# A redrawn first phase, and eight row blocks of the second graph layer done with seven block products instead of eight

## The chip, the cores and the metric

The kernel runs on one core of a Trainium2 chip. Its time is device time in microseconds (us) of one execution. Before the change the median of three runs is 610.74 us (609.37 to 611.44). Engines are named as the profile names them: PE is TensorE's matmul, PEld its weight load, DVE VectorE, ACT ScalarE, POOL GpSimd, SP the queue that issues most transfers.

## The reference, cut to what matters

There are 3327 nodes with 256 features and a dense symmetric 0/1 adjacency `adj` with about 1% ones. Two residual graph layers follow each other, each on `h = relu(layernorm(x))`:

```python
# layer 0 (adj_a = adj_b = adj)
attn_a = sigmoid([adj @ h, h] @ Wa.T + ba); attn_b = sigmoid([adj @ h, h] @ Wb.T + bb)
g = h @ W_sa;  e = where(adj != 0, exp(-leaky_relu(s_left[:, None] + s_right[None, :], 0.01)), 0)
x = x + sigmoid(attn_a * (e / (e.sum(1) + 1e-5)) @ g + attn_b * (adj @ (h @ W_gcnb) + b_gcnb))
# layer 1, h taken anew from x
a_norm = dinv * (adj + I) * dinv
x = x + relu((a_norm @ h + h) @ W + b)
```

## The kernel before, in words

Nodes are padded to 26 tiles of 128, handled as 13 pairs (`PAIRS`); a pair has tiles e = 0, 1. `m` is a pair of output rows and `u` the pair of nodes that is summed over. Every fp32 operand of a product is split into a 16-bit first half and a 16-bit rest (`HI` and `LO`, `HI1` and `LO1`, `Z` read as bf16 and `E2`), so one product costs two or three matmuls. Order within an engine is written by hand and engines meet at semaphores only.

*First phase.* For s = 0..12 PE runs `dense(s)` (h times both weight matrices, 12 matmuls of 512 columns into `accA[1]`), `turn(s + 2)` (four fp32 transposes), for s from 6 on `neighbours(0, s - 6)`, from 7 on `unit(0, s - 7)`, and `project(s + 1)` (8 matmuls of 18 or 12 columns, each with its own weights). DVE takes the mean and variance of x (`row_stats`), makes the second halves (`turned_second`, `second_halves`) and the scores; POOL makes the inverse deviations in eight batches (`BATCHES`), a batch when all its pairs' statistics are there; ACT normalises. `load_adj(m, c)` on POOL brings the adjacency rows of pair m in two chunks (6 and 7 pairs wide) into `stage`, and `turn_adj(m, c)` on DVE turns a chunk with two stream transposes into `adjT[m % 2]`; a load waits until the chunk before it in the same place has been turned.

*Layer 0.* For every m and u, ACT makes `leaky` and `expo` of 128x512 scores, DVE `mask` (times the adjacency) and `split`, PE `unit(m, u)` (12 matmuls of 257 or 256 columns into `accE`) and, for the next m, `neighbours(m + 1, u - 6)` (8 matmuls of 260 or 258 columns). A ring of 8 buffers of `Z` lets ACT and DVE run ahead. Between m = 0 and m = 1 PE runs all of `neighbours(1, u)` and then waits in `unit(1, 0)` for `row_sums(0)` on DVE, which empties `accE` and adds what `with_bias(0)` on POOL has made. `with_bias(0)` stands behind `load_adj(3, 0)` and the small operation `nbias` in POOL's order.

*Layer 1.* `dense1(m)` makes h times W for pair m (`HI1`, `LO1`). `pooled(k, u)` adds four tiles' products for output pair `ORDER[k]`: 8 matmuls of 256 columns, 104 for one k. The transposed adjacency comes back from `adjT_store` into three buffers `adj1[k % 3]`. POOL makes the node's own term (`self_term(k)`: add, two scalings, add), DVE adds it (`pooled_out`), takes relu and residual and ACT issues the store. Blocks k = 0, 1, 2 are interleaved while the last `dense1` are made, k = 3..11 follow each other, and k = 12 is done tile by tile (`pooled_tile`).

Of the kernel before, what the change touches and what calls it, by code (L numbers as in the profile page):

```python
# [12 lines left out]
P = 128  # L13
QUAD = 32
# [5 lines left out]
def gnn_kernel(nc, x, adj, W_sa, a_sa, W_g, b_g, Wa, ba, Wb, bb, W1, b1, out):  # L20
# [14 lines left out]
    BATCHES = [(0, 1), (1, 2), (2, 3), (3, 4), (4, 5), (5, 7), (7, 9), (9, PAIRS)]  # L35
# [6 lines left out]

    def chunk_of(u):
        return [c for c, (a, b) in enumerate(CHUNKS) if a <= u < b][0]

    def batch_of(i):
        return [n for n, (a, b) in enumerate(BATCHES) if a <= i < b][0]

# [3 lines left out]
    with ExitStack() as ctx:  # L52
# [100 lines left out]

        def bank(t, e):
            return t[:, 512 * e:512 * e + 512]
# [94 lines left out]
        tile_done = sem("tile_done")  # L250
        y_ok = sem("y_ok")
        o_ok = sem("o_ok")
        o_out = [sem("o_out0"), sem("o_out1")]

# [30 lines left out]
        def _(sp):  # L285
# [20 lines left out]
            def keep_adj(m):  # L306
                sp.wait_ge(tr_ok, NC * (m + 1))
                sp.dma_start(adjT_store[m], adjT[m % 2][:].rearrange("p u e i v -> p (u e i v)").bitcast(U32)
                             ).then_inc(stored[m % 2], 16)
# [3 lines left out]

            sp.wait_ge(adj_in[1], adj_count(1, 1))
            spread_left(0)
# [19 lines left out]
            sp.wait_ge(tr_ok, NC * PAIRS)  # L335
# [11 lines left out]
        def _(pool):  # L347
# [9 lines left out]
            def load_adj(m, c):  # L357
                u0, u1 = CHUNKS[c]
                if m >= 1:
                    pool.wait_ge(tr_ok, NC * (m - 1) + c + 1)  # L360
# [15 lines left out]
            def inv_stds(n):  # L376
                a, b = BATCHES[n]
                pool.wait_ge(stats, b)
                pool.tensor_tensor(ve[:, a:b], mv[:, a:b, :, 1], epss[:, 0:b - a], ALU.add).then_inc(vplus, 1)
                pool.wait_ge(vplus, n + 1)  # L380
                pool.tensor_tensor(rstd[:, a:b], ve[:, a:b], halfs[:, 0:b - a], ALU.pow).then_inc(rstd_ok, 1)
# [33 lines left out]
            inv_stds(0)  # L415
            inv_stds(1)
            pool.wait_ge(pads, 1)
            load_adj(0, 0)
            inv_stds(2)
            score_weight_parts()  # L420
            load_adj(0, 1)
            loads = {6: (1, 0), 7: (1, 1), 11: (2, 0), 12: (2, 1)}
            for s in range(PAIRS):
                score_parts(s)
                if s == 0:
                    inv_stds(3)
                if s in (0, 1, 2, 4):
                    inv_stds({0: 4, 1: 5, 2: 6, 4: 7}[s])
                gate_columns(s)
                if s in loads:  # L430
                    load_adj(*loads[s])

# [27 lines left out]
            pool.wait_ge(bias_in, 32)  # L460
            pool.tensor_scalar(nbias[:], bias2[:], -1.0, None, ALU.mult).then_inc(nbias_ok, 1)
# [13 lines left out]
            def self_term(k):  # L475
# [6 lines left out]
                pool.wait_ge(hp_ok, k + 1)  # L482
                pool.wait_ge(selfw_ok, 1)
                for e in range(2):
                    t = 2 * ORDER[k] + e
                    ins = pool.tensor_scalar(hpw[:, e], hp[:, e], selfw[:, t:t + 1], None, ALU.mult)
                ins.then_inc(hpw_c, 1)
# [3 lines left out]

            for k in range(PAIRS):
                self_term(k)

        @block.scalar
        def _(act):
# [8 lines left out]
            def norm(i):  # L505
                act.wait_ge(x_in[group_of(i)], x_count(group_of(i)))
                act.wait_ge(nmr_ok, batch_of(i) + 1)
# [6 lines left out]
            def turned(i):  # L514
                act.wait_ge(hT_ps, i + 1)
                if i >= 2:
                    act.wait_ge(dn_ps, 2 * i - 2)
# [8 lines left out]
            def first_halves(i):  # L526
                src = dn[:].rearrange("p (e k d) -> p e k d", e=2, k=2)
                for e in range(2):
                    act.wait_ge(dn_ps, 2 * i + e + 1)
                    dst = bass.AP(HI[:].tensor, (2 * i + e) * HIW, [[TILES * HIW, P], [G0, 2], [1, D]])  # L530
                    act.activation(dst, src[:, e], ACT.Copy).then_inc(hi_ok, 1)
# [79 lines left out]
            for s in range(PAIRS + 7):  # L611
                if s == 0:
                    first_halves(0)
                if s + 1 < PAIRS:
                    turned(s + 1)
                if s + 2 < PAIRS:
                    norm(s + 2)
                if 0 <= s - 6 < PAIRS:
                    expo(0, s - 6)
                if 0 < s < PAIRS:  # L620
                    first_halves(s)
                if s == 1:
                    left_first()
                if 0 <= s - 5 < PAIRS:
                    leaky(0, s - 5)
                if s == 11:
                    first_weights(2)
            act.wait_ge(srw_ok, PAIRS)
            act.activation(el[:], srw[:, :, 3], ACT.Exp, scale=SLOPE).then_inc(el_ok, 1)
            gate_exp(0)  # L630
            gated_b(0)

            for m in range(1, PAIRS):
                for u in range(PAIRS + 1):
                    if u == 1 and m >= 2:
                        norm1(m - 2)
                    if u == 2 and m >= 2:
# [3 lines left out]
                    if u == 7:  # L641
                        half_tanh(m - 1)
                    if u == 9:
                        gate_exp(m)
                    if u == 12:
# [3 lines left out]
                    if u >= 1:  # L649
                        expo(m, u - 1)  # L650
            norm1(LAST - 1)
# [5 lines left out]
            rounded1(LAST)  # L657
            first_halves1(LAST)

# [19 lines left out]

            for k in range(PAIRS):  # L680
                store_out(k)
            act.wait_ge(o_out[0], out_count(LAST, 0))
# [3 lines left out]
        def _(pe):  # L686
# [42 lines left out]
            def dense(i):  # L729
# [3 lines left out]
                for e in range(2):  # L733
                    if i >= 1:
# [14 lines left out]
            def neighbours(m, u):  # L749
                if u in [a for a, _ in CHUNKS]:  # L750
                    pe.wait_ge(tr_ok, NC * m + chunk_of(u) + 1)
# [82 lines left out]

            def pooled_tile(k, e):
# [21 lines left out]
            for s in range(PAIRS):  # L857
                dense(s)
                if s == 0:
                    turn(1)  # L860
                    project(0)
                    spread_weights(2, 4, 2)
                    keep_busy(4)
                if s == 1:
                    widen_first()
                if s + 2 < PAIRS:
# [3 lines left out]
                if s >= 6:  # L870
                    neighbours(0, s - 6)
                if s >= 7:
                    unit(0, s - 7)
                if s + 1 < PAIRS:
                    project(s + 1)
            for u in range(PAIRS - 6, PAIRS):
                neighbours(0, u)
                unit(0, u - 1)
            unit(0, LAST)
            for u in range(PAIRS):  # L880
# [26 lines left out]
            for u in range(2, 5):  # L907
                pooled(2, u)
            dense1(LAST)
            for u in range(5, 8):  # L910
# [6 lines left out]
            for k in range(3, LAST):  # L917
                for u in range(PAIRS):
                    pooled(k, u)
            for e in range(2):  # L920
# [3 lines left out]
        def _(dve):  # L924
# [15 lines left out]
            def minus_mean(n):  # L940
                a, b = BATCHES[n]
                dve.wait_ge(rstd_ok, n + 1)
                dve.scalar_tensor_tensor(out=nmr[:, a:b], in0=mv[:, a:b, :, 0], scalar=-1.0, in1=rstd[:, a:b],
# [61 lines left out]
            def second_halves(i):  # L1005
                for e in range(2):
                    dve.wait_ge(hi_ok, 2 * i + e + 1)
                    first = bass.AP(HI[:].tensor, (2 * i + e) * HIW, [[TILES * HIW, P], [G0, 2], [1, D]])
                    dve.tensor_tensor(LO[:, 2 * i + e, 0:2 * D].rearrange("p (k d) -> p k d", k=2),
                                      bank(dn, e).rearrange("p (k d) -> p k d", k=2), first,  # L1010
                                      ALU.subtract).then_inc(lo_ok, 1)

            def turn_adj(m, c):
# [9 lines left out]
                for e in range(2):  # L1023
                    src = stage[:, e].bitcast(U32).rearrange("p b (u r) -> p b u r", r=QUAD)[:, :, u0:u1]
# [246 lines left out]
```

## Time and profile before

| | |
|---|---|
| median of three runs | 610.74 us |
| the profiled execution, its own time | 611.8 us |
| its span in the profile | 610.0 us |
| granted TensorE clock, mean over the span | 0.993 |
| PE / PEld busy | 593.4 / 508.4 us |
| DVE / ACT / POOL busy | 425.2 / 362.4 / 255.5 us |

The 1.8 us between the execution's own time and its span lie around the profile. PE busy counts pipelined matmuls with their whole latency, so how much PE does is better read from the spacing of starts; where the timeline shows starts at an even spacing, that spacing is the cost of one.

### The profile page before, as it was taken

To read this page: it belongs to the slowest core of one execution; us is meant where nothing else is said; L and a number is where in the kernel's file an instruction comes from. 1 tells how busy PE (TensorE), PEld (TensorE's weight loads), DVE (VectorE), ACT (ScalarE), POOL (GpSimd) and SP (SyncE) were. 2 spreads that over 40 slices of the span, in tenths; PEclk is the share of its full clock that TensorE was granted. 3 is DMA by queue.
4 is the path that set the end of the run, shared out by engine and by line. 5 is a ranking of instruction groups with operands and counts; after the bars stand their busy time and mean duration, and the time that the engine had idled before them with its cause. 6 is when DMAs were issued, how large, how long until landed. Compare 5 with 4: busy or idle time off the path is not lost.

```text
span 610.0 us, 13250 instructions
## 1 busy us (share of the span) xinstructions
PE 593.4 (97%) x5265; PEld 508.4 (83%) x5265; DVE 425.2 (70%) x811; ACT 362.4 (59%) x878; POOL 255.5 (42%) x361
## 2 busy tenths in 40 slices
PE   7889998999999999999999999999999999999996
PEld 5446687888888888888888888888888888888886
DVE  6897885999998999899989989988753121111111
ACT  3687667797887979797979788979642000000000
POOL 3664313554453435343525276313132374435433
PEclk8999999899999999999999999999999999999999
DMA  8908399957566565647474745010400486546401
GB/s 198 225 3 113 111 134 249 203 83 182 94 150 121 123 134 110 146 98 162 81 177 67 190 52 79 2 19 1 130 2 18 113 318 215 174 157 193 144 20 35
DMA packets 55801, 73.60 MB, mean 121 GB/s; under 512 B 20027, under 2 KB 47933, under 8 KB 54331
## 3 DMA queue, kind: packets, MB, share of 16 engines
q0 software_dynamic: 28544, 22.15, 26.5%
q1 hardware_dynamic: 24754, 46.42, 23.5%
q10 hardware_dynamic: 2441, 4.20, 2.2%
q8 instruction: 41, 0.67, 0.4%
q14 instruction: 21, 0.17, 0.1%
HBM read 69.31 MB, written 22.16 MB: 150 GB/s over the span
## 4 chain that ended last, share of the span: by engine, by line
PE 82%; DVE 5%; DMA 4%; issue 4%; POOL 4%; ACT 2%; ACTq 0%; POOLq 0%; DVEq 0%
PE accE L786 11%; PE accE L788 11%; PE accE L787 11%; PE accA L764 10%; PE accA L765 10%; PE accA L831 7%; PE accA L830 7%; PE accE L830 4%; PE accE L831 4%; DMA stage<-in_adj_dram 3%; POOL stage L369 1%; DVE bst L933 1%; PE pw L803 1%; PE accA L847 1%; PE pw L805 1%
## 5 line engine op out<-in xcount | busy, mean ns | idle before, releaser
L786 PE MATMUL accE<-HI,Z 128*128 128x257 f16 x676 | 185.2, 274 | 2.4 <-DVE wm L1078 2.1
L788 PE MATMUL accE<-HI,E 128*128 128x257 f16 x676 | 184.8, 273 | 0.0
L787 PE MATMUL accE<-LO,Z 128*128 128x256 f16 x676 | 184.7, 273 | 0.0
L549 ACT ACTIVATE Z<-LO,sr 128x256 f32<-128x256 f32 x338 | 151.4, 497 | 35.6 <-PE accE L788 35.6
L764 PE MATMUL accA<-HI,adjT 128*128 128x260 f16 x676 | 154.0, 273 | 0.0
L765 PE MATMUL accA<-LO,adjT 128*128 128x258 f16 x676 | 154.0, 273 | 0.0
L558 ACT ACTIVATE Z<-Z,sr 128x256 f32<-128x256 f32 x338 | 150.1, 496 | 0.2
L1034 DVE TENSOR_TENSOR Z<-adjT,Z 128x512 f32<-128x512 bf16 x169 | 127.0, 751 | 17.1 <-ACT Z L558 16.1
L1040 DVE TENSOR_TENSOR E<-Z 128x512 bf16<-128x512 f32 x169 | 129.0, 763 | 5.8
L369 POOL DMA_DIRECT2D stage<-in_adj_dram x96 | 59.3, 649 | 93.0 <-DVE adjT L1026 88.6
L831 PE MATMUL accA<-LO,adjT 128*128 128x256 f16 x416 | 91.6, 273 | 0.0
L830 PE MATMUL accA<-HI,adjT 128*128 128x256 f16 x416 | 91.6, 273 | 0.0
L786 PEld LDWEIGHTS accE<-HI,Z 128*128 128x128 bf16 x676 | 66.0, 98 | 11.6 <-issue 2.3
L764 PEld LDWEIGHTS accA<-HI,adjT 128*128 128x128 bf16 x676 | 65.8, 97 | 9.2
L787 PEld LDWEIGHTS accE<-LO,Z 128*128 128x128 bf16 x676 | 66.2, 98 | 8.7
L788 PEld LDWEIGHTS accE<-HI,E 128*128 128x128 bf16 x676 | 66.0, 98 | 8.8
L765 PEld LDWEIGHTS accA<-LO,adjT 128*128 128x128 bf16 x676 | 65.8, 97 | 8.8
L1026 DVE STREAM_TRANSPOSE adjT<-stage 128x768 uint32<-128x768 uint32 (+1 forms) x52 | 51.0, 1017 | 1.1 <-DMA stage<-in_adj_dram 1.1
L448 POOL TENSOR_SCALAR wx<-wx 128x512 f32<-128x512 f32 x13 | 12.6, 968 | 81.8 <-ACT wx L584 81.8
L830 PE MATMUL accE<-HI,stage 128*128 128x256 f16 x208 | 45.7, 273 | 0.0
L831 PE MATMUL accE<-LO,stage 128*128 128x256 f16 x208 | 45.7, 272 | 0.0
L830 PEld LDWEIGHTS accA<-HI,adjT 128*128 128x128 bf16 x416 | 40.7, 98 | 4.7
(127 smaller groups left out, 721.0 us busy)
## 6 DMA issues: line engine op xcount, KB each, us to landing
adjT_store<-adjT SPq DMA_DIRECT2D x11, 1664.0 KB, 6.3
stage<-in_adj_dram POOLq DMA_DIRECT2D x48, 192.0 KB, 5.0
stage<-in_adj_dram POOLq DMA_DIRECT2D x36, 224.0 KB, 5.2
adjT<-adjT_store SPq DMA_DIRECT2D x7, 896.0 KB, 6.0
adjT<-adjT_store SPq DMA_DIRECT2D x7, 768.0 KB, 6.0
stage<-adjT_store SPq DMA_DIRECT2D x4, 896.0 KB, 6.4
stage<-adjT_store SPq DMA_DIRECT2D x4, 768.0 KB, 5.8
out_dram<-late ACTq DMA_DIRECT2D x11, 256.0 KB
```

The source lines that it names most:

```text
L369: pool.dma_start(stage[32 * b:32 * b + 32, :, :, w0:w1_], src).then_inc(adj_in[c], 16)
L549: ins = act.activation(Z[:, n % RING, v], slw[:, m], ACT.Relu, bias=sr99[:, t:t + 1], scale=1.0 - SLOPE)
L558: ins = act.activation(Z[:, n % RING, v], Z[:, n % RING, v], ACT.Exp, bias=sr01[:, t:t + 1], scale=-1.0)
L764: pe.matmul(dst[:, 0:D + 4], w, HI[:, t, ONE:HIW], start=(t == 0), stop=False)
L765: ins = pe.matmul(dst[:, 2:D + 4], w, LO[:, t, D:LOW], start=False, stop=(t == TILES - 1))
L786: pe.matmul(dst[:, 0:D + 1], zhi, HI[:, t, 0:D + 1], start=(t == 0), stop=False)
L787: pe.matmul(dst[:, 0:D], zhi, LO[:, t, 0:D], start=False, stop=False)
L788: ins = pe.matmul(dst[:, 0:D + 1], zlo, HI[:, t, 0:D + 1], start=False, stop=(t == TILES - 1))
L830: pe.matmul(dst, w, HI1[:, t, :], start=(t == 0), stop=False)
L831: ins = pe.matmul(dst, w, LO1[:, t, :], start=False, stop=(t == TILES - 1))
L1034: dve.tensor_tensor(Z[:, n % RING], rows, Z[:, n % RING], ALU.mult).then_inc(mask_ok, 1)
L1040: dve.tensor_tensor(E2[:, n % RING], Z[:, n % RING], hi, ALU.subtract).then_inc(e2_ok, 1)
```

## The change

The first phase is put in another order. Statistics are made pair by pair (`inv_std(i)`, `minus_mean(i)`, one `row_stats` a step, four ahead). The second half of `dense(0)` and `dense(1)` comes behind `turn(1)` and `turn(2)`, `project(0)`. `turn_adj` does one transpose at a time and stands at steps 4 to 7 and 11 to 14. `unit(0, u)` moves from step u + 7 to u + 10, `neighbours` stay at u + 6; the steps go on to 22 and take `neighbours(1, 0..3)` with them. `nbias` moves to the front of POOL's order; `gate_args(0)`, `gates(0)`, both chunks of `turn_adj(2, ·)` and `row_sums(0)` go into the loop over u of m = 1 (at u = 1, 3, 2 and 4, 7 and 9, and 6).

In layer 1 the blocks k = 4..11 (`SEVEN`) take two pairs of nodes (a "duo", 6 of them) as a 2x2 block product: two output tiles, two summed pairs, two halves of 128 columns. Seven products of 128 columns stand in the place of eight, by sums made beforehand: `TH`, `TL` of the node values (once), `SA` of the adjacency (per block: three sums on DVE, one on POOL, in two parts). The thirteenth pair keeps its 8 matmuls of 256 columns. `output_seven` puts the products together. The scaling in the own term moves from POOL to ACT.

```diff
-            def inv_stds(n):
-                a, b = BATCHES[n]
-                pool.wait_ge(stats, b)
+            def inv_std(i):
+                pool.wait_ge(stats, i + 1)
...
             pool.wait_ge(consts, 5)
-            inv_stds(0)
-            inv_stds(1)
+            inv_std(0)
+            inv_std(1)
             pool.wait_ge(pads, 1)
             load_adj(0, 0)
-            inv_stds(2)
+            inv_std(2)
             score_weight_parts()
             load_adj(0, 1)
-            loads = {6: (1, 0), 7: (1, 1), 11: (2, 0), 12: (2, 1)}
+            pool.wait_ge(bias_in, 32)
+            pool.tensor_scalar(nbias[:], bias2[:], -1.0, None, ALU.mult).then_inc(nbias_ok, 1)
+            inv_std(3)
+            inv_std(4)
+            loads = {6: (1, 0), 8: (1, 1)}
...
+            def adj_difference(k, part):
+                adj_sums_wait(pool, k, part)
+                w0, w1 = PARTS[part]
+                pool.tensor_tensor(combos(k, 2, w0, w1), duo_adj(k, 0, 0, w0, w1), duo_adj(k, 0, 1, w0, w1),
+                                   ALU.subtract).then_inc(s3_ok, 1)
+
             for k in range(PAIRS):
+                if k + 1 in SEVEN:
+                    for part in range(2):
+                        adj_difference(k + 1, part)
                 self_term(k)
...
+            def pooled_seven(k):
+                pe.wait_ge(y_ok, 2 * (k - 2))
...
+                        for n, (weights, hi, lo) in enumerate((
+                                (adjs[0], HI1[:, ta, H[0]], LO1[:, ta, H[0]]),
+                                (adjs[1], HI1[:, tb, H[0]], LO1[:, tb, H[0]]),
+                                (sums[3], HI1[:, tb, H[1]], LO1[:, tb, H[1]]),
+                                (sums[1], TH[:, b, v, H[1]], TL[:, b, v, H[1]]),
+                                (adjs[3], TH[:, b, v, H[0]], TL[:, b, v, H[0]]),
+                                (None, None, None),
+                                (sums[0], TH[:, a, v, H[0]], TL[:, a, v, H[0]]),
+                                (sums[2], TH[:, a, v, H[1]], TL[:, a, v, H[1]]))):
...
-            turns = {5: (0, 0), 6: (0, 1), 10: (1, 0), 11: (1, 1)}
+            turns = {4: (0, 0, 0), 5: (0, 0, 1), 6: (0, 1, 0), 7: (0, 1, 1),
+                     11: (1, 0, 0), 12: (1, 0, 1), 13: (1, 1, 0), 14: (1, 1, 1)}
...
+            def adj_sums(k, part):
+                n = 2 * (k - SEVEN[0]) + part + 1
+                adj_sums_wait(dve, k, part)
+                w0, w1 = PARTS[part]
+                dve.tensor_tensor(combos(k, 0, w0, w1), duo_adj(k, 0, 1, w0, w1), duo_adj(k, 1, 1, w0, w1),
+                                  ALU.add).then_inc(s1_ok, 1)
...
+            for k in SEVEN:
+                output_seven(k)
+                if k + 2 in SEVEN:
+                    for part in range(2):
+                        adj_sums(k + 2, part)
```

## Rows read from the trace of the kernel before

**Rows 1.** The page: busy time of each engine; a group of ACT (busy us, mean ns).
```profile
PE 593.4 (97%) x5265; PEld 508.4 (83%) x5265; DVE 425.2 (70%) x811; ACT 362.4 (59%) x878; POOL 255.5 (42%) x361
...
L549 ACT ACTIVATE Z<-LO,sr 128x256 f32<-128x256 f32 x338 | 151.4, 497 | 35.6 <-PE accE L788 35.6
```
**Rows 2.** Waits of PE: who was waited for, us in total, times, longest.
```profile
PE tp L690 <- DVE hTx L990: 3.0, 5, 0.9
PE accE L786 <- DVE wm L1078: 2.1, 1, 2.1
```
**Rows 3.** PE's timeline in layer 1 (start, length): blocks 3 to 11, then 12.
```profile
491.55 0.27 PE L830 MATMUL accA<-HI,adjT 128*128 128x256 f16 x1
...
593.73 0.27 PE L846 MATMUL accA<-HI,adjT 128*128 128x256 f16 x1
```
**Rows 4.** PE's timeline in step 5 and 6 of the first phase.
```profile
39.67 0.63 PE L690 MATMUL tp<-ident,hf 128*128 128x128 f32 x4 [0.67 <-DVE hTx L990]
40.14 0.17 PE L718 MATMUL pw<-w6s,hTx 128*128 128x18 bf16 x1
...
40.34 0.38 PE L738 MATMUL accA<-wh,hTx 128*128 128x512 f16 x1
...
42.71 0.38 PE L740 MATMUL accA<-wh,hTx 128*128 128x512 f16 x1
```
**Rows 5.** Weight loads in the same 0.2 us, PEld's timeline.
```profile
40.17 0.10 PEld L718 LDWEIGHTS pw<-w6s,hTx 128*128 128x128 f16 x1
40.19 0.10 PEld L720 LDWEIGHTS pw<-w6s,hTx 128*128 128x128 f16 x1
```
**Rows 6.** Groups of DVE by line, 12 to 50 us: busy us, mean ns of one.
```profile
L1009 DVE TENSOR_TENSOR LO<-accA,HI 128x512 f16<-128x512 f32 x16 | 10.3, 682 | 1.3 <-ACT HI L531 1.3
L933 DVE BATCH_NORM_STATS2 bst<-xs 128x6 f32<-128x256 f32 x22 | 8.2, 411 | 0.0
L1026 DVE STREAM_TRANSPOSE adjT<-stage 128x768 uint32<-128x768 uint32 (+1 forms) x4 | 3.9, 1018 | 0.0
```
**Rows 7.** PE's timeline: first matmul of `dense(7)` and of `dense(12)`.
```profile
45.21 0.38 PE L738 MATMUL accA<-wh,hTx 128*128 128x512 f16 x1
...
73.01 0.38 PE L738 MATMUL accA<-wh,hTx 128*128 128x512 f16 x1
```
**Rows 8.** Between m = 0 and 1: DVE's, POOL's and ACT's timelines.
```profile
89.37 1.84 DVE L1026 STREAM_TRANSPOSE adjT<-stage 128x768 uint32<-128x768 uint32 x2 [1.09 <-DMA stage<-in_adj_dram]
91.50 2.39 POOL L369 DMA_DIRECT2D stage<-in_adj_dram  x4 [12.16 <-DVE adjT L1026]
94.28 0.48 ACT L567 ACTIVATE eg<-zg,nbias 128x2 f32<-128x2 f32 x2 [7.31 <-POOL nbias L461]
95.27 1.85 POOL L440 TENSOR_SCALAR wm<-bgrep,gate 128x256 f32<-128x256 f32 x2 [1.09 <-DVE gate L1057]
97.21 1.27 POOL L444 TENSOR_TENSOR wm<-wm,ub 128x512 f32<-128x512 f32 x1
106.52 0.27 PE L786 MATMUL accE<-HI,Z 128*128 128x257 f16 x1 [2.06 <-DVE wm L1078]
```
**Rows 9.** Windows: busy of PE, PEld, DVE, ACT, POOL, then PEclk, DMA share, GB/s.
```profile
106.50:110.10 3.60, 3.58 (x19) 2.60 (x20) 3.57 (x5) 3.41 (x9) 1.42 (x3) 0.55 0.28 118
```
**Rows 10.** POOL's and DVE's timelines, where they meet and where not (498 us).
```profile
449.32 1.28 POOL L444 TENSOR_TENSOR wm<-wm,ub 128x512 f32<-128x512 f32 x1
449.37 1.78 DVE L1040 TENSOR_TENSOR E<-Z 128x512 bf16<-128x512 f32 x1
486.20 1.59 POOL L481 TENSOR_TENSOR late<-HI,LO 128x512 f32<-128x512 f16 x1 [1.15 <-DVE wx L1213]
498.10 1.15 POOL L481 TENSOR_TENSOR late<-HI,LO 128x512 f32<-128x512 f16 x1 [1.04 <-DVE wx L1213]
```
**Rows 11.** Around `dense1(12)`: PE waits in all; DVE's timeline before it.
```profile
PE pw L803 <- DMA hTx<-hfx: 0.2, 1, 0.2
471.87 0.69 DVE L1098 TENSOR_TENSOR hfx<-hf,hfx 128x512 f16<-128x512 f32 x1 [1.87 <-ACT hfx L598]
```

More of the change, by code:

```diff
@@ L733, in dense @@
                 for e in range(2):
+                    if i <= 1 and e == 1:
+                        turn(i + 1)
+                    if i == 1 and e == 1:
+                        project(0)
                     if i >= 1:
@@ L869, in _ @@
                     keep_busy(4)
[L870 to L874, printed above, removed]
-                    project(s + 1)
[L876 to L880, printed above, removed]
+                if s >= SUMS_BEHIND:
+                    neighbours(0, s - SUMS_BEHIND)
+                if s > BEHIND:
+                    unit(0, s - BEHIND - 1)
+                if s >= 2 and s + 1 < PAIRS:
+                    project(s + 1)
+            for s in range(PAIRS, PAIRS + BEHIND + 1):
+                n = s - SUMS_BEHIND
+                neighbours(n // PAIRS, n % PAIRS)
+                unit(0, s - BEHIND - 1)
+            for u in range(BEHIND + 1 - SUMS_BEHIND, PAIRS):
                 neighbours(1, u)
@@ L906, in _ @@
                 pooled(2, u)
-            for u in range(2, 5):
+            for u in range(2, 7):
                 pooled(2, u)
             dense1(LAST)
-            for u in range(5, 8):
+            for u in range(7, 8):
                 pooled(2, u)
@@ L916, in _ @@
                 pooled(2, u)
-            for k in range(3, LAST):
+            for k in range(3, SEVEN[0]):
                 for u in range(PAIRS):
                     pooled(k, u)
+            for k in SEVEN:
+                pooled_seven(k)
             for e in range(2):
@@ L1003, in diagonal_first, with second_half, turn_adj @@
                 ins.then_inc(diag_ok, 1)
[L1005 to L1013, printed above, removed]
+            def second_half(i, e):
+                dve.wait_ge(hi_ok, 2 * i + e + 1)
+                first = bass.AP(HI[:].tensor, (2 * i + e) * HIW, [[TILES * HIW, P], [G0, 2], [1, D]])
+                dve.tensor_tensor(LO[:, 2 * i + e, 0:2 * D].rearrange("p (k d) -> p k d", k=2),
+                                  bank(dn, e).rearrange("p (k d) -> p k d", k=2), first,
+                                  ALU.subtract).then_inc(lo_ok, 1)
+            def turn_adj(m, c, e):
                 u0, u1 = CHUNKS[c]
@@ L1129, in _ @@
             row_stats(2)
+            second_half(0, 0)
+            minus_mean(2)
+            turned_second(1)
+            second_half(0, 1)
             dve.wait_ge(w1_in, 16)
@@ new lines, in _ @@
+            row_sums(LAST)
+            rounded_second1(LAST - 1)
+            second_halves1(LAST - 2)
+            row_stats1(LAST)
+            exact_columns(0)
+            second_halves1(LAST - 1)
+            minus_mean1(LAST)
+            column_sums(0)
+            rounded_second1(LAST)
+            degrees()
+            exact_columns(1)
+            column_sums(1)
+            exact_columns(2)
+            second_halves1(LAST)
+            second_combos(0)
+            output(0)
+            column_sums(2)
@@ L1245, in _ @@
+            second_combos(1)
+            output(1)
+            second_combos(2)
+            for k in range(SEVEN[0], SEVEN[0] + 2):
+                for part in range(2):
+                    adj_sums(k, part)
+                output(k - 2)
+            for k in SEVEN:
+                output_seven(k)
+                if k + 2 in SEVEN:
+                    for part in range(2):
+                        adj_sums(k + 2, part)
             for e in range(2):
```

366 lines of the change are left out of this document (259 added, 107 removed).

## The prediction

> **What bounds the kernel now.** I read the page first, then PE's waits, then timelines of four stretches. The page shows PE busy 97% of the span and DVE 70% [rows 1], and the mean clock is 0.993. PE's waits are few: in the whole trace 3.0 us for the turned second halves, 2.1 us once for `row_sums(0)`, and little else [rows 2]. So from about 50 us to 605 us the kernel costs what its matmuls cost, but for one gap, and a change pays only by taking matmul time away (layer 1's seven products) or by filling PE's gaps before 50 us and at 104 us (the redrawn front).
>
> **Layer 1, PE.** Blocks 3 to 11 take 102.18 us from first to first matmul [rows 3]: 11.35 us a block, 109.2 ns for each of 104 matmuls of 256 columns. In the front the twelve of 512 columns start 215.5 ns apart (eleven gaps in 2.37 us) [rows 4]. The line through both gives 56.0 ns for 128 columns. The bounds: half of the 256 column price is 54.6 ns from below; from above the four fp32 transposes of 128 columns, 0.47 us together, 117 ns each [rows 4]. I take 56, since both 16-bit widths lie on one line. What could hold a short matmul back is its own weight load, as every matmul has one: `project` starts eight matmuls in 0.2 us [rows 4], with the loads some 25 ns apart though one load is 0.10 us long [rows 5]. So loads overlap each other and 56 ns leaves them room. A block of seven has 6 duos x 2 tiles x 7 products x 2 halves = 168 matmuls of 128 columns and 8 of 256: 168 x 0.0560 + 8 x 0.1092 = 10.28 us, 1.07 less than 11.35. Eight blocks: 8.6 us (10.4 at 54.6 ns).
>
> **Layer 1, what must keep up.** In the block's 10.28 us DVE has the three sums in two parts (six operations on 768 bf16 elements), the putting together (about 1.9 us that read PSUM, by 256 column operations of some 0.4 us) and two scaled adds and the final one, 1.5 us, that read two SBUF tensors. POOL has two differences, the add and the bias add. These two engines shut each other out: a DVE operation of commonly 0.69 us took 1.78 beside POOL's one of 1.28, ending 0.55 us behind it, and POOL's add took 1.59 us where a DVE operation ran, 1.15 alone [rows 10]. So their two-tensor operations must be added up. POOL: 1.15 us for 512 elements makes 1.7 us for 768; 2 x 1.7 + 1.15 + 1.27 (the row of the same size) = 5.8 us [rows 8, 10]. DVE's sum of 768 elements has no row. Mixed-width operations on 512 elements take 0.68 us whatever their width [rows 6], about 0.15 of it fixed; by elements 768 cost 0.95 us, by bytes (all three tensors are 16 bits wide, which no row is) 0.55. Together with 1.5 and 5.8 us: 13.0 us a block by elements, 10.6 by bytes. Sums for blocks 6 to 11 are made from the end of block 4 on, and the last part of block 11's is wanted 6 x 10.28 + 5.6 = 67.3 us later. 6 x 10.6 = 64 us is in time, 6 x 13.0 = 78 is 10.7 us late. I take the 0.55, as the judgement that halving all widths counts for something, and keep 0.95 as a rival; this is the point where the forecast is least backed by rows.
> The Trainium skill, "VectorE: DVE Perf Modes", section "Mode 2×_1P — pack two bf16 into one 32-bit read", says that a two-tensor operation handles two elements a cycle if all are 16 bits wide and step by one. As an estimate from that page a sum would be 0.55 us and layer 1's gain 8.6 us; at one element a cycle the 10.7 us above would be lost. No run here shows it yet.
>
> **Layer 1, the way in.** DVE gets `exact_columns`, `column_sums` and `second_combos` three times: 2048, 4 x 512 and 2048 elements, 2.2 + 2.7 + 2.3 = 7.2 us, 22 us in a stretch (450 to 503 us) where it is nearly idle. The first piece stands before `rounded_second1(12)`, whose transfer `dense1(12)` is waiting for by 0.2 us now [rows 11]. The 2.2 us fall into DVE's wait for ACT and the 2.7 us overlap the wait of 1.87 us, so about 1 us is left over; `dense1(12)` stands 1.75 us later in PE's order (two `pooled` of 0.87). Cost nothing; without that cover 1 to 3 us. The own scaling on ACT costs nothing: ACT is idle there.
>
> **The front up to dense(12).** Per step DVE will have 0.6 + 1.2 us of second halves (three operations of 0.68, of which neighbours overlap by 0.08), 0.95 of statistics and 0.2 of small ones, and 0.9 to 1.05 for a transpose at four steps [rows 6]: 3.0 and 4.0 us. PE's step is 2.59 + 0.45 + 0.2 = 3.25 us, and 4.13 with `neighbours`. Before, two statistics a step made DVE's step 4 to 4.7 us. Walking the queues: `dense(1)` starts some 2 us sooner, as `turned_second(1)` no longer stands behind `largest(3)`; but then the statistics of pair 3 wait on POOL behind `load_adj(0, 1)` (issue 2.4 us), and POOL's single powers of 0.7 us stand behind `gate_columns`. I get `dense(2)` at 23.2 us, `dense(4)` at 32.9, and `dense(7)` at 45.2, which is where it is now [rows 7], since the four transposes fill steps that statistics filled, then 4.15, 4.13, 4.13, 5.44 and 4.99 us a step, so `dense(12)` starts at 68.1 and ends at 70.7 us. Now it starts at 73.01 [rows 7] and ends at 75.6. Three `unit` of 1.315 us, 3.95 us, have been put off, so the real gain here is 0.9 us. From below it could be -1 (the walk has an error of 1 us at each end), from above 4.
>
> **The gap at 104 us.** Before, ACT waited 7.31 us for `nbias`, which stood behind `load_adj(3, 0)`, which waited for a transpose, which waited for its transfer until 89.37; unit(1, 0) began at 106.52, after 2.06 us of waiting [rows 8], and then 3.6 us ran at a mean clock of 0.55, which costs 1.6 us more [rows 9]. The change takes `nbias` out of that chain. What is late next: `with_bias(0)` still stands behind `load_adj(3, 0)`, and that now waits for the second transpose of `turn_adj(2, 0)`, at u = 4 of m = 1. Counted from the end D of `dense(12)`: ACT's `leaky` and `expo` are four activations of 0.497 us that overlap by 0.09 [rows 1], 1.6 us, and 1.74 where each waits for the one before, as in m = 0; they end m = 0 at D + 16.8, DVE, with three transposes more in its way, at D + 18.4; masks of m = 1 go at ACT's 1.6 us, with the gates' small steps between, the transpose at u = 4 ends at D + 27.5, the issue of the load (2.4 us) at D + 30.2, `with_bias` (1.85 + 1.27) at D + 33.4, the emptied `accE` at D + 34.4. PE has 0.9 + 1.3 + ten steps of 2.2 + nine `neighbours` of 0.885: D + 32.2. So a gap of 2.2 us stays, with the same drop of clock behind it. `unit(1, 0)` begins at 70.7 + 34.4 = 105.1 against 106.52: the front as a whole gives 1.4 us. If the chain comes 2.2 us sooner the gap and its clock are gone, 3.7 us more.
>
> **Sum.** The profiled execution took 611.8 us; 611.8 - 8.6 - 1.4 = 601.8. It lay 1.06 above the median, which gives 610.74 - 10.0 = 600.7 us.
>
> **Rivals.**
> *Shut out (no gain, or slower).* DVE's sums go by elements: +10.7 us, 611.4; with each lost handover between the engines 616. For it: the rows show nothing faster than one element a cycle. Against: no row has three 16-bit tensors. It eats all of the gain from 0.93 us a sum on, and starts to cost at 0.65.
> *Weight load bound (slower).* In a long stream of short matmuls with weights at a step of two elements the load no longer overlaps. At the row's 98 ns a matmul, 168 x 0.098 + 0.87 = 17.3 us a block, +6.0 x 8: 657 us. It decides against the change from 56 + 10.0/1344 = 63 ns on. Against it: loads 25 ns apart [rows 5], though only in bursts of eight.
> The Trainium skill, "TensorE: Matmul & The Clock Gate", section "Back-to-back issue gap", gives about 81 ns per matmul of 128 columns in a stream of pairs of load and matmul. As an estimate from that page, a block would cost 14.5 us and the kernel 634. Its figure for 512 columns, about 131 ns, is far under this trace's 215.5, so I trust it little.
> *The front gives nothing or costs.* The chain through `load_adj(3, 0)` or a late transfer makes the gap 3 us longer than I have it, or the early steps slip: 602 to 605.
>
> **How the numbers follow.** Chances: forecast 0.65 (598 to 603.5); front worse 0.14 (to 606); shut out 0.14 (608 to 616); load bound 0.05; both front gains and cheaper matmuls 0.02 (under 598). A difference of 0.3%, 1.8 us, is about what measurement can tell from none. Faster: 0.65 + 0.14 + 0.02 and 0.02 of the shut-out case, 0.83; same 0.07 and slower 0.10, out of the rest. The range 597 to 609.5 leaves out the load bound and most of the upper half of shut out.
>
> **What would show it.** Starts in `pooled_seven` 56 ns apart, blocks 4 to 11 at 10.3 us; no wait of PE for the sums; DVE's sum at 0.55 us undisturbed; PE's wait for `wm` near 2 us once, at about 103 us, with a clock drop; `dense(12)` at 68. Wrong if matmuls come slower than 60 ns, or PE waits for DVE or POOL from block 6 on.

## The result and the profile after

The changed kernel took 618.67 us (median of 5 runs, 618.23 to 620.64), the kernel before 611.4 us on the same chip (609.37 to 611.47): ratio 1.0134, 95% interval 1.0114 to 1.0154. It is slower by 1.3%, where 600.7 us, 1.7% faster, was forecast with a range of 597 to 609.5. The profiled execution took 618.23 us, its span is 616.4 us (before 610.0).

The page of the changed kernel, which answers to [rows 1]:

```profile
PE 588.4 (95%) x5842; PEld 509.7 (83%) x5842; DVE 526.4 (85%) x930; ACT 381.1 (62%) x915; POOL 267.7 (43%) x361
```

PE is busy 5 us less, and no longer fills the span. The seven products save it more than that, as the block times below show: its busy time also counts matmuls that ran at the slow clock. DVE has gone from 425 to 526 us. PE's waits, answering to [rows 2] (who was waited for, us in total, times, longest):

```profile
PE accA L966 <- DVE LO L1424: 6.2, 4, 3.5
PE accE L881 <- DVE wm L1216: 5.0, 2, 2.9
...
PE accE L966 <- DVE LO L1424: 1.1, 1, 1.1
```

L966 is the first product of a part in `pooled_seven` and L1424 the last of DVE's three sums: 7.3 us in all. L881 is `unit`, which waits for `accE` to be emptied: now twice, 2.9 and 2.1 us, before once, 2.1 us.

**Where layer 1's time goes.** PE's timeline (start, length), four places of it: a run of undisturbed products, block 6 where the wait is longest, the start of block 10, and the start of block 12:

```profile
599.79 0.22 PE L966 MATMUL accE<-HI,stage 128*128 128x128 f16 x1
599.85 0.22 PE L967 MATMUL accE<-HI,stage 128*128 128x128 f16 x1
599.90 0.22 PE L966 MATMUL accE<-HI,LO 128*128 128x128 f16 x1
...
533.00 0.29 PE L966 MATMUL accA<-HI,adjT 128*128 128x128 f16 x1 [3.54 <-DVE LO L1424]
...
577.04 0.27 PE L940 MATMUL accA<-HI,adjT 128*128 128x256 f16 x1
...
579.20 0.23 PE L966 MATMUL accA<-HI,adjT 128*128 128x128 f16 x1 [1.12 <-DVE LO L1424]
...
600.13 0.27 PE L984 MATMUL accA<-HI,adjT 128*128 128x256 f16 x1
```

The first three lines stand 0.05 to 0.06 us apart. The eight blocks of seven products start at 507.37, 518.17, 528.42, 544.99, 555.24, 565.49, 577.04 and 588.59, and block 12 at 600.13. So they take 10.80, 10.25, 16.57, 10.25, 10.25, 11.55, 11.55 and 11.54 us, 92.76 together. Before, the same eight blocks took 8 x 11.35 = 90.8 us [rows 3]. An undisturbed block is 10.25 us. PE waits for a sum in five blocks: 0.37 us in block 4, 3.54 in block 6, and 1.11 or 1.12 in each of the last three. Behind the wait at block 6 the clock fell to 1.2 GHz for at least 4 us (windows; columns as in [rows 9], PEclk is the 0.50):

```profile
533.00:537.00 4.00, 4.00 (x38) 4.00 (x39) 3.93 (x3) 0.00 (x0) 3.35 (x2) 0.50 0.18 67
```

Now one period of the two engines that feed PE. DVE's timeline from one part's first sum to the next block's:

```profile
575.35 1.51 DVE L1418 TENSOR_TENSOR LO<-adjT 128x768 bf16<-128x768 bf16 x1
576.89 0.56 DVE L1421 TENSOR_TENSOR LO<-LO,adjT 128x768 bf16<-128x768 bf16 x1
577.49 1.65 DVE L1424 TENSOR_TENSOR LO<-adjT,LO 128x768 bf16<-128x768 bf16 x1
579.06 1.99 DVE L1418 TENSOR_TENSOR LO<-adjT 128x768 bf16<-128x768 bf16 x1
581.09 1.88 DVE L1421 TENSOR_TENSOR LO<-LO,adjT 128x768 bf16<-128x768 bf16 x1
583.00 0.56 DVE L1424 TENSOR_TENSOR LO<-adjT,LO 128x768 bf16<-128x768 bf16 x1
583.48 0.28 DVE L1434 TENSOR_TENSOR ub<-accA,ub 128x128 f32<-128x128 f32 x1
...
586.28 0.69 DVE L1454 SCALAR_TENSOR_TENSOR late<-wm,xs 128x512 f32<-128x512 f32 x1
586.89 1.51 DVE L1418 TENSOR_TENSOR LO<-stage 128x768 bf16<-128x768 bf16 x1
```

and POOL's over the same time:

```profile
574.78 1.66 POOL L530 TENSOR_TENSOR late<-HI,LO 128x512 f32<-128x512 f16 x1 [3.78 <-DVE wx L1450]
577.46 1.26 POOL L532 TENSOR_TENSOR late<-late,b1rep 128x512 f32<-128x512 f32 x1 [1.02 <-ACT late L723]
578.68 3.87 POOL L538 TENSOR_TENSOR LO<-stage 128x768 bf16<-128x768 bf16 x2
586.33 1.66 POOL L530 TENSOR_TENSOR late<-HI,LO 128x512 f32<-128x512 f16 x1 [3.78 <-DVE wm L1450]
```

The period is 586.89 - 575.35 = 11.54 us, just the length of PE's last blocks, and DVE has no idle time in it: DVE sets the pace. A sum is 0.56 us if left alone (two of the six). The other four last 1.51 to 1.99, and each ends right behind a POOL operation: 576.86 behind 576.44, 579.14 behind 578.72, 581.05 and 582.97 behind the two differences, the second of which ends at 582.55. Then follow 3.4 us of putting together and output (583.48 to 586.89), in which POOL is idle until 586.33: it waits for DVE's `y_ok` (the 3.78 us). So nearly all of POOL's work falls on DVE's sums and none beside the operations that read PSUM. Six sums at a spacing of 0.59 and 3.4 make 6.9 us; the other 4.6 DVE stands still for POOL.

**Where the front's time goes.** PE's timeline at the two gaps, answering to the last line of [rows 8]:

```profile
110.02 0.27 PE L881 MATMUL accE<-HI,Z 128*128 128x257 f16 x1 [2.89 <-DVE wm L1216]
...
140.88 0.27 PE L881 MATMUL accE<-HI,Z 128*128 128x257 f16 x1 [2.09 <-DVE wm L1216]
```

Before, unit(1, 0) began at 106.52 after its 2.06 us of waiting, and unit(2, 0) without a wait:

```profile
136.80 0.27 PE L786 MATMUL accE<-HI,Z 128*128 128x257 f16 x1
```

POOL's and then DVE's timeline ahead of both gaps:

```profile
103.27 2.39 POOL L417 DMA_DIRECT2D stage<-in_adj_dram  x4 [19.66 <-DVE adjT L1165]
105.58 1.96 POOL L491 TENSOR_SCALAR wm<-bgrep,gate 128x256 f32<-128x256 f32 x2
107.62 1.26 POOL L495 TENSOR_TENSOR wm<-wm,ub 128x512 f32<-128x512 f32 x1
...
118.13 2.46 POOL L417 DMA_DIRECT2D stage<-in_adj_dram  x4 [9.24 <-DVE adjT L1165]
```

```profile
109.00 0.88 DVE L1216 SCALAR_TENSOR_TENSOR wm<-accE,rsg,wm 128x256 f32<-128x256 f32 x2 [2.70 <-POOL wm L495]
...
129.49 2.10 DVE L1165 STREAM_TRANSPOSE adjT<-stage 128x896 uint32<-128x896 uint32 x2 [1.92 <-DMA stage<-in_adj_dram]
```

The first gap is the one that was forecast: `with_bias(0)` behind `load_adj(3, 0)`, and DVE stands 2.70 us for it. The second was not. `load_adj(3, 1)` is issued at 118.13, 9.4 us later than before (108.69), because it waits for `turn_adj(2, 1)`, which the change moved behind `row_sums(0)`, to u = 7 and 9. Its data land at 129.49 with DVE waiting. The same load on POOL and the same two transposes on DVE, before the change:

```profile
108.69 2.48 POOL L369 DMA_DIRECT2D stage<-in_adj_dram  x4 [10.21 <-DVE adjT L1026]
...
125.67 2.09 DVE L1026 STREAM_TRANSPOSE adjT<-stage 128x896 uint32<-128x896 uint32 x2
```

They ran at 125.67 without a wait. `minus_mean1(0)` stands behind them on DVE since the change, and `norm1(0)` on ACT behind that (ACT's timeline):

```profile
133.04 1.09 ACT L644 ACTIVATE hf<-xs,nmr,rstd 128x256 f32<-128x256 f32 x2 [4.95 <-issue]
```

The masks of m = 2 stand behind it, and `row_sums(1)` behind the masks.

### The profile page after: what moved, and what is told of

It is laid out like the page before. It is cut to its first block, busy times and chain, and to the rows that moved or that the text cites. A ratio compares the mean times of both kernels' runs of the same rounds, so it can differ in the third digit from the quotient of the medians.

```text
span 616.4 us, 14657 instructions
## 1 busy us (share of the span) xinstructions
PE 588.4 (95%) x5842; PEld 509.7 (83%) x5842; DVE 526.4 (85%) x930; ACT 381.1 (62%) x915; POOL 267.7 (43%) x361
## 4 chain that ended last, share of the span: by engine, by line
PE 60%; DVE 19%; issue 6%; DMA 4%; ACT 3%; POOL 2%; DVEq 0%; ACTq 0%; POOLq 0%
PE accE L881 10%; PE accE L883 10%; PE accE L882 10%; PE accA L859 10%; PE accA L860 9%; DMA stage<-in_adj_dram 4%; DVE LO L1418 4%; DVE LO L1421 3%; DVE HI L1412 1%; DVE adjT L1165 1%; PE accA L984 1%; PE accA L985 1%; POOL stage L417 1%; PE accA L833 1%; PE accA L835 1%
## 5 line engine op out<-in xcount | busy, mean ns | idle before, releaser
L881 PE MATMUL accE<-HI,Z 128*128 128x257 f16 x676 | 184.3, 273 | 5.5 <-DVE wm L1216 5.0
L1178 DVE TENSOR_TENSOR E<-Z 128x512 bf16<-128x512 f32 x169 | 130.8, 774 | 5.8
L881 PEld LDWEIGHTS accE<-HI,Z 128*128 128x128 bf16 x676 | 65.8, 97 | 15.1 <-issue 5.7
L859 PEld LDWEIGHTS accA<-HI,adjT 128*128 128x128 bf16 x676 | 65.8, 97 | 9.2
L723 ACT ACTIVATE late<-late,selfw 128x256 f32<-128x256 f32 x26 | 11.8, 500 | 94.9 <-POOL late L530 94.9
L530 POOL TENSOR_TENSOR late<-HI,LO 128x512 f32<-128x512 f16 x13 | 21.0, 1616 | 46.2 <-DVE wm L1450 15.8
L966 PE MATMUL accA<-HI,LO 128*128 128x128 f16 x240 | 41.1, 225 | 0.0
L966 PE MATMUL accA<-HI,adjT 128*128 128x128 f16 x180 | 34.2, 225 | 6.2 <-DVE LO L1424 6.2
L925 PE MATMUL accA<-HI,adjT 128*128 128x256 f16 x156 | 34.8, 272 | 0.2 <-DVE LO L1242 0.2
```

Source lines behind the costliest of these rows:

```text
L859: pe.matmul(dst[:, 0:D + 4], w, HI[:, t, ONE:HIW], start=(t == 0), stop=False)
L881: pe.matmul(dst[:, 0:D + 1], zhi, HI[:, t, 0:D + 1], start=(t == 0), stop=False)
L966: pe.matmul(dst, weights, hi, start=False, stop=False)
L1178: dve.tensor_tensor(E2[:, n % RING], Z[:, n % RING], hi, ALU.subtract).then_inc(e2_ok, 1)
```

## Experiments

Times are medians. The ratio to the kernel before on the same chip, with its 95% interval, counts; one profile of each kernel gives the starts on PE.

**Each half alone.** `e1_second_only` has the front of before and all that belongs to the seven products; `e2_front_only` has the new front and the eight products of before.

> The front as before, layer 1 as in the changed kernel. If both halves of the change cost what their stretches of the changed trace show (blocks 4 to 11 take 92.8 us there against 90.8 before), this is 2 us slower than before: about 613.5. If the seven products gave the 8.6 us that their matmuls are worth and the loss is all the front's, it is 602 to 603.

> The redrawn front, layer 1 as before. Block 4 begins 4.5 us later in the changed trace than in the one before, 1.5 us of it ahead of the first dense and perhaps chance. If the front is guilty: 614.5 to 616, with two waits of the first unit of m = 1 and m = 2 for row_sums. If it is innocent (only the start of that run was late): 610 to 612.

Measured: the second half alone 613.4 us, 1.0044 (1.0028 to 1.0061); the front alone 615.91 us, 1.0075 (1.005 to 1.0099). Both cost, some 3 and 5 us, and together they make the 7 to 8 us of the whole. In the first PE waits 0.39 us in block 4, 3.55 us in block 6 and 1.12 or 1.13 in each block after it, PE's timeline:

```profile
526.88 0.23 PE L951 MATMUL accA<-HI,adjT 128*128 128x128 f16 x1 [3.55 <-DVE LO L1395]
...
538.43 0.23 PE L951 MATMUL accA<-HI,adjT 128*128 128x128 f16 x1 [1.12 <-DVE LO L1395]
```

So the front has no part in them. One thing differs: here the clock did not fall behind block 6, which took 13.98 us and not 16.57, but blocks 7 and 8 took 11.55 us each and not 10.25. The eight blocks take 92.82 us, in the whole change 92.76. So the slow clock cost layer 1 nothing: while PE was slow, DVE got ahead, and the next two blocks had no wait. In the second, PE waits 1.40 us before unit(1, 0) and 2.77 before unit(2, 0).

**The difference taken off POOL.** POOL's `adj_difference` goes to DVE, so that POOL has no operation on the adjacency left, and DVE two more of them a block.

```diff
-                if k + 1 in SEVEN:
-                    for part in range(2):
-                        adj_difference(k + 1, part)
                 self_term(k)
...
                 dve.tensor_tensor(combos(k, 0, w0, w1), duo_adj(k, 0, 1, w0, w1), duo_adj(k, 1, 1, w0, w1),
                                   ALU.add).then_inc(s1_ok, 1)
+                dve.tensor_tensor(combos(k, 2, w0, w1), duo_adj(k, 0, 0, w0, w1), duo_adj(k, 0, 1, w0, w1),
+                                  ALU.subtract).then_inc(s3_ok, 1)
```

> The changed kernel with the difference of the adjacency made on VectorE, two operations a block more there and two less (3.9 us) on POOL. Theory shut out (VectorE's sums wait for POOL's operations, 4.8 us a block): sums go at 0.59 us, VectorE needs 3.4 + 8 x 0.59 + about 2 of waiting = 10.2 us a block, blocks come every 10.25 to 10.3 us, the whole is 8 to 11 us faster than the changed kernel, 608 to 610. Rival, VectorE simply has too much work of its own: two operations more make each block longer, 11.6 to 12.8 us, 619 to 628.

> The front as before and layer 1 with the difference on VectorE. If both theories hold (shut out, guilty front) this is the fastest of the four: 611.4 - 8.6 = 602 to 604, below both kernels. If the front is innocent it equals the run before it. If VectorE is overloaded: 614 and more.

Measured: with the new front 606.99 us, 0.9932 (0.9911 to 0.9953), somewhat below the 608 to 610 us that was expected; with the front of before 602.38 us, 0.9865 (0.9834 to 0.9897). In both PE waits for no sum, and all eight blocks take 10.25 or 10.26 us. More work on DVE, and DVE is done sooner: its timeline in the first of the two kernels,

```profile
541.61 1.51 DVE L1415 TENSOR_TENSOR LO<-stage 128x768 bf16<-128x768 bf16 x1
543.05 0.55 DVE L1417 TENSOR_TENSOR LO<-stage 128x768 bf16<-128x768 bf16 x1
543.52 0.55 DVE L1420 TENSOR_TENSOR LO<-LO,stage 128x768 bf16<-128x768 bf16 x1
544.10 1.51 DVE L1423 TENSOR_TENSOR LO<-stage,LO 128x768 bf16<-128x768 bf16 x1
...
547.05 0.56 DVE L1423 TENSOR_TENSOR LO<-stage,LO 128x768 bf16<-128x768 bf16 x1
548.44 0.29 DVE L1433 TENSOR_TENSOR ub<-accA,ub 128x128 f32<-128x128 f32 x1 [0.83 <-ACT ub L761]
```

Eight operations end at 547.61, 6.0 us after the first began, of which two are long beside `self_term`. With 3.4 us for the output that is 9.4 us a block, and 0.83 us is left over for waiting. Of the two ways to see the loss (DVE has too much work; POOL stops DVE) the first falls.

**One difference taken off POOL.** As above, but for the first part alone.

```diff
-                    for part in range(2):
-                        adj_difference(k + 1, part)
+                    adj_difference(k + 1, 1)
...
+                if part == 0:
+                    dve.tensor_tensor(combos(k, 2, w0, w1), duo_adj(k, 0, 0, w0, w1), duo_adj(k, 0, 1, w0, w1),
+                                      ALU.subtract).then_inc(s30_ok, 1)
```

> The changed kernel with only the difference of the first part on DVE, that of the second still on POOL. If POOL's and DVE's two-tensor operations add up, DVE's period falls from 11.55 us by one POOL difference (1.9) and rises by one DVE operation (0.55), to 10.2 us, just under PE's 10.25: the steady waits of 1.1 us a block are gone, the blocks are 10.25 to 10.35 us, and only a part of the wait of 3.5 us at block 6 is left (0 to 2 us). 609 to 612 us. Rival (it is the order on POOL, a late start of the difference behind self_term, and not the added lengths): each block still waits 0.5 us or more, 613 to 616 us.

Measured: 612.02 us, 1.0008 (0.9986 to 1.003). The wait at block 6 is 1.30 us (block 11.73), and the blocks after it take 10.55 or 10.56 us, PE's timeline at two starts:

```profile
562.34 0.27 PE L940 MATMUL accA<-HI,adjT 128*128 128x256 f16 x1
...
572.89 0.27 PE L940 MATMUL accA<-HI,adjT 128*128 128x256 f16 x1
```

DVE is still what binds, by 0.3 us a block and not, as expected, just under PE. With two, one and no difference on POOL DVE's period is 11.55, 10.55 and 9.4 us. The first two are measured with DVE never idle; the third is its 10.25 us less the 0.83 of waiting, as PE sets the pace there. Each difference on POOL costs DVE about 1.1 us net: the sum beside it stands still for 1.3 to 1.4 us (1.88 and 1.99 against 0.56), and DVE saves some 0.4 us of its own (the next operation starts 0.47 us behind its difference, at 543.05 and 543.52 above). Not tried was to leave both on POOL and place them beside the operations that read PSUM.

**The first gap.** From here on the difference is on DVE. `e5_bias_ahead_of_load` keeps the new front and swaps two lines on POOL.

```diff
-            load_adj(3, 0)
             with_bias(0)
+            load_adj(3, 0)
```

> The changed kernel with the difference on DVE (607.0 us, 0.993 of before) and one swap on POOL: with_bias(0) ahead of load_adj(3, 0). Theory (the first gap is set by with_bias(0) queued behind the issue of load_adj(3, 0), 2.4 us): PE's wait of 1.8 us before unit(1, 0) goes to under 0.5, unit(1, 0) starts 1.3 to 1.8 us sooner, and load_adj(3, 0) is issued hardly later, since it waits for a transpose until then. The second gap, before unit(2, 0), has another cause and stays or grows to 2 to 3.5 us, so that unit(2, 0) starts 0 to 1.5 us sooner: 605.5 to 607 us. Rival (the gap is set by the gates of block 0, which the change moved into block 1, so that POOL would wait for gate_ok in any order): the wait stays at 1.5 us or more and the time at 607.

Measured: 606.23 us, 0.9927 (0.9906 to 0.9948), not to be told from the 0.9932 without the swap. PE's timeline:

```profile
108.81 0.27 PE L878 MATMUL accE<-HI,Z 128*128 128x257 f16 x1 [0.90 <-DVE wm L1213]
...
140.53 0.27 PE L878 MATMUL accE<-HI,Z 128*128 128x257 f16 x1 [2.94 <-DVE wm L1213]
```

The first wait fell from 1.79 us to 0.90, not to under 0.5. DVE no longer waits for POOL there; what is left is DVE's own queue, in which `row_sums(0)` at u = 6 stands behind six masks of m = 1, two transposes and a wait of 1.41 us for the transfer of adj(2, 0). The second gap grew by what the first lost. The expected time, 605.5 to 607 us, came out although the wait did not.

**The second gap.** `e6_and_transposes_sooner` also puts both transposes of `turn_adj(2, 1)` at u = 5, ahead of `row_sums(0)`.

```diff
-                    if m == 1 and u in (7, 9):
-                        turn_adj(2, 1, (u - 7) // 2)
+                    if m == 1 and u == 5:
+                        turn_adj(2, 1, 0)
+                        turn_adj(2, 1, 1)
```

> The kernel of the swap, with the two transposes of turn_adj(2, 1) before row_sums(0), at u = 5 of m = 1 and no longer at u = 7 and 9. Theory (the second gap comes from load_adj(3, 1), which is issued 9 us later than before because it waits for those transposes): load_adj(3, 1) is issued by 110 us, its transfer has landed before DVE asks for it, and PE's wait of 2.0 us before unit(2, 0) is gone, as is DVE's wait for the transfer (1.9 us). unit(2, 0) starts some 2 us sooner than with the swap alone: 603.5 to 605.5 us. Rival (the wait comes from norm1(0) and gated_b(1) moved to u = 1 to 4 of m = 2 on ACT, or from minus_mean1(0)): DVE no longer waits for the transfer but PE still waits 1.5 us or more, and the time is that of the swap alone.

Measured: 606.62 us, 0.9935 (0.9917 to 0.9952), where 603.5 to 605.5 was expected. The cause of the second gap is shown: `load_adj(3, 1)` is issued at 108.53 us, DVE does not wait for its data, and unit(2, 0) has no wait. But the transposes (2.09 us) now stand ahead of `row_sums(0)`, and the first gap is 3.11 us:

```profile
111.12 0.27 PE L878 MATMUL accE<-HI,Z 128*128 128x257 f16 x1 [3.11 <-DVE wm L1213]
```

The sum of the two gaps is 3.8, 3.84 and 3.11 us in the three kernels: DVE's four transposes of pair 2 had no free place between the masks of m = 1 in any of the three orders, each of which put them ahead of one `row_sums` or the other. The time of the whole did not move.

**`nbias` alone.** `e8_second_and_bias_sooner` has the front of before, the seven products, the difference on DVE, and one thing of the new front: `nbias` is made early.

```diff
             load_adj(0, 1)
+            pool.wait_ge(bias_in, 32)
+            pool.tensor_scalar(nbias[:], bias2[:], -1.0, None, ALU.mult).then_inc(nbias_ok, 1)
...
             load_adj(3, 0)
-            pool.wait_ge(bias_in, 32)
-            pool.tensor_scalar(nbias[:], bias2[:], -1.0, None, ALU.mult).then_inc(nbias_ok, 1)
             with_bias(0)
```

> The front of before with the seven products and the difference on DVE (602.4 us, 0.9865 of before), and nbias made right behind load_adj(0, 1) on POOL and no longer behind load_adj(3, 0). Theory (the wait of ACT for nbias, 7 us, made row_sums(0) late): ACT's ub comes sooner, but with_bias(0) stays behind load_adj(3, 0), and the second step is what ended last (1.85 + 1.27 us on POOL behind the load), so unit(1, 0) starts 0 to 0.9 us sooner: 601.5 to 602.5 us, ratio 0.985 to 0.987. Rival (ub itself is the last thing that POOL's addition of the bias waits for): the gap of 0.9 to 2.1 us and its drop of clock go, and it takes 600 to 601 us.

Measured: 600.49 us, 0.9843 (0.9822 to 0.9863), the lowest of all, and as the rival had it: PE has no wait between 80 and 460 us. The time alone doesn't show that the edit helped, as e4 without it had 0.9865 (0.9834 to 0.9897); and counted from the first `dense`, unit(2, 0) comes only 0.3 us sooner than in e4, whose wait was 0.86 us and had no slow clock behind it. What the edit shows is which chain made the gap, and there the rival's reason was wrong too. The POOL and DVE timelines of e8:

```profile
94.94 1.96 POOL L490 TENSOR_SCALAR wm<-bgrep,gate 128x256 f32<-128x256 f32 x2
96.98 1.27 POOL L494 TENSOR_TENSOR wm<-wm,ub 128x512 f32<-128x512 f32 x1
```

```profile
97.03 1.77 DVE L1156 TENSOR_TENSOR Z<-adjT,Z 128x512 f32<-128x512 bf16 x1 [3.34 <-ACT Z L606]
...
104.07 0.87 DVE L1200 SCALAR_TENSOR_TENSOR wm<-accE,rsg,wm 128x256 f32<-128x256 f32 x2
```

`with_bias(0)` starts only 0.3 us sooner than before (94.94 against 95.27) and is done at 98.25, 5.8 us before DVE asks for it. It was not what ended last in the kernel before either: there it was done at 98.48 [rows 8] and DVE's `wm` began at 105.50, without waiting for POOL. DVE's timeline before the change:

```profile
98.72 0.69 DVE L1034 TENSOR_TENSOR Z<-adjT,Z 128x512 f32<-128x512 bf16 x1 [3.34 <-ACT Z L558]
...
105.50 0.88 DVE L1078 SCALAR_TENSOR_TENSOR wm<-accE,rsg,wm 128x256 f32<-128x256 f32 x2
```

The first mask of m = 1 began at 98.72 and `wm` at 105.50; in e8 at 97.03 and 104.07. What `nbias` held was ACT's queue: behind `gate_exp(0)` stand `leaky` and `expo` of m = 1, behind these DVE's masks, and behind four masks `row_sums(0)`.

## Why the prediction was wrong

The step that failed is the one on what must keep up in layer 1: DVE's sums were to be in time (a period of 10.6 us, begun at the end of block 4), and the waits there were put at nothing. The runs showed a period of 11.54 us, begun 5.5 us late, and layer 1 cost 1.9 us where it was to give 8.6. The second miss is the front, which was to give 1.4 us and alone cost some 5 (e2). The parts one by one:

**Layer 1, PE: right.** 10.28 us a block was predicted, 10.25 measured where nothing is waited for; (10.25 - 8 x 0.1092) / 168 is 55.8 ns a matmul, predicted 56.0. Eight such blocks are 82.0 us where it was 90.8 (e3, e4, e8): the gain of 8.6 to 8.8 us is there. The weight load bound is out.
The figure of 81 ns from the Trainium skill, "TensorE: Matmul & The Clock Gate", section "Back-to-back issue gap", does not hold in this stream of loads and matmuls; what that section gives for an isolated matmul, N / 2.4 + 2.5 ns, comes to 55.8 ns and does.

**Layer 1, DVE's sum: right.** The least backed number, 0.55 us for 768 bf16 elements, is 0.55 to 0.56 where POOL is quiet. The Trainium skill's rule for two packed 16-bit operands, cited in the prediction, agrees.

**Layer 1, what must keep up: the step that failed.** The prediction added 5.8 us of POOL, 1.5 of DVE and six sums of 0.55 to 10.6 us and let 1.9 us of PSUM operations overlap POOL. Two things were off.

First, the period. The term put at nothing, the 1.9 us, is there in full: POOL waits for DVE's `y_ok` while DVE puts together, so its four operations all meet sums, as the two timelines above show. POOL's difference is 1.9 us, not 1.7. On the other side POOL's four operations, counted at 5.8 us, make DVE stand still for 4.6. So the period is 6.9 + 4.6 = 11.54 us. At 10.6 it was already longer than PE's 10.28, and the sums were held to be in time only by their head start.

Second, the head start. The sums for block 6 were to begin at the end of block 4 (518.17). DVE was 5.5 us late there, by the trace of the changed kernel:

```profile
523.69 0.29 DVE L1434 TENSOR_TENSOR ub<-accA,ub 128x128 f32<-128x128 f32 x1 [2.15 <-ACT ub L764]
```

It began `output_seven(4)` behind block 5's sums, `output(3)` until 521.5 and 2.15 us for ACT's first product, which stands on ACT behind the store of block 3 and so behind `output(3)` itself. One of its scaled adds then met POOL's differences, and the two of that block took 2.92 us and not 0.88. So block 6, the first whose sums could not be made ahead, waited 3.54 us.

From 523.69 on DVE is never idle until the first part of block 11's sums is ready, at 590.68. PE would have taken that part at 580.5 at 10.25 us a block; 5.5 of the 10.2 us that it is late are the late start, 2.0 the long scaled adds, and the rest the longer period. This is the whole loss of layer 1 but for 0.55 us at block 4: 92.76 - 82.0 = 10.8 us, so +1.9 us where -8.6 was predicted. 2.8 us of slow clock lie within it and added nothing, as e1 without them shows. The rival "shut out" had the right mechanism and place, but its condition, a sum by elements, was not what it takes; that its price of 10.7 us came so near 10.8 is chance.

The Trainium skill, "SBUF — State Buffer", section "Who interferes with whom", says that a DVE instruction with two SBUF inputs contends with a GpSimd instruction that reads SBUF, and that the shared port pair is an exclusive lock.
The trace agrees: a sum of 0.56 us lasts 1.5 to 2.0 us and ends 0.4 us behind POOL's operation.

**Layer 1, the way in: right for PE.** `dense1(12)` waits 0.2 us for its transfer as before [rows 11]. The operations are longer beside POOL than taken (`second_combos` once 3.24 us), and they are part of DVE's lateness at block 4.

**The front up to dense(12): right to dense(7), then off by a term.** The first `dense` started 1.48 us later in this profile (14.02 against 12.54; it waited 2.68 us for a transfer of weights, before 1.78). That is no effect of the change: over all kernels it starts at 12.5 to 15.9 us with the old front and 12.7 to 14.4 with the new. With it, dense(2), dense(4) and dense(7) stand at 24.76, 34.51 and 46.61, and 23.2, 32.9 and 45.2 were predicted: 1.4 to 1.6 apart each time. dense(12) stands at 71.28, where 68.1 + 1.5 = 69.6 would be right. 1.0 us of the missing 1.7 are three waits of PE at 57.1, 58.9 and 60.7 for second halves. Ahead of them ACT is idle for 2.9 us until 55.73, though PE's result is there by 53.5; the trace names no engine for it. All six kernels with the new front have such a stop of 2.1 to 3.8 us there, and the four with the old front have none. Its cause is open. So dense(12) comes 57.26 us after the first `dense`, before 60.47, 3.2 us sooner (over all kernels 56.6 to 58.0 with the new front, 59.9 to 60.7 with the old), against 3.95 us of `unit` put off: "the real gain here is 0.9 us" is a loss of about 0.7.

**The gap at 104 us: forecast for the changed kernel, misread for the one before.** `with_bias(0)` behind the load does end last in the new front: unit(1, 0) at D + 36.1, forecast D + 34.4, a wait of 2.9 against 2.2. But in the old front it did not, and [rows 8] showed it: it was done at 98.48, PE's wait ended at 106.52. Taking `nbias` out removed the gap there without any other edit (e8). What that is worth is small and not settled: the gap was 2.06 us with a slow clock behind it in the profile before, but 0.85 and 0.86 without one in e1 and e4, which have the same front. The new front moved gates and transposes into m = 1 and so made a new gap in place of the old.

**The gap at 140 us: missed.** The rival "the front gives nothing or costs" named a late transfer, but not which. The prediction costed what each moved transpose does to DVE, and not what waits for it on POOL: `load_adj(3, 1)`, then its transfer, the transposes of pair 3, `minus_mean1(0)`, `norm1(0)`, the masks, `row_sums(1)`. 2.1 us, and in e3 another 1.7 of slow clock. From e4 to e3 the front costs unit(2, 0), counted from the first `dense`, 4.4 us: 1.15 up to dense(12), 0.9 in the first gap, 2.0 in the second, 0.2 in `unit(0, 0)`'s wait, which leaves 0.15.

Together: the profiled span grew by 6.4 us, of which unit(2, 0) carries 4.1 (1.5 of it the later start), layer 1 1.9, and 0.4 lie between.

## What to carry to other kernels

Where two engines shut each other out as DVE and POOL do here, which of their operations meet is decided by the semaphores between them: draw one period of both before anything is counted as overlapping. A share of DVE's work given to POOL cost DVE more than it saved, as POOL's operation was over three times as long (1.9 us against 0.56); try it all on one engine. For a chain of handed-over pieces check where the engine that makes them stands when the chain begins, and the first deadline as well as the last. A slow clock or a wait on PE costs nothing where another engine sets the pace: add up that engine's chain. Follow each moved instruction to whoever waits for it on every queue, the issue of the next transfer above all. A queue's head that waits (`gate_exp(0)` for `nbias`) is priced by what stands behind it on its own engine, not by the chain of its own result.

## What was not expected of the hardware

A wait of 2 to 3.5 us on PE is not always followed by the lower clock. The same wait at block 6 was followed by slow matmuls in one profile (3.54 us, block 16.57) and not in another (3.55 us, block 13.98). Before unit(1, 0) a wait of 2.06 us (before) and of 2.50 us (e7) had it, with a mean clock of 0.55 [rows 9] and 0.53, and waits of 2.89 us (after) and 3.11 us (e6) had none, at 1.00. Before unit(2, 0) it is the same: 2.01 us (e3) had it, at 0.53, and 2.09 (after), 2.77 (e2) and 2.94 us (e5) had none. The waits of 0.85 to 1.79 us at these two places had none. Windows of the changed kernel and of e7 right behind the gap:

```profile
110.02:113.60 3.58, 3.58 (x33) 3.18 (x34) 2.49 (x4) 2.07 (x5) 0.00 (x0) 1.00 0.02 2
```

```profile
110.40:114.00 3.60, 3.58 (x18) 2.57 (x19) 2.18 (x3) 0.92 (x3) 0.00 (x0) 0.53 0.01 2
```

So among waits of 2.0 to 3.6 us the length does not tell whether the clock drops, and one profile can't price it: it is 1.7 us behind a gap in the front, where PE sets the pace (11.77 us from unit(1, 0) to the next `unit`, 10.10 without), or nothing.
